# Six gathered tiles a step instead of seven in the first sweep of a graph network, and 36 counted batches in seven steps

## What is computed

```python
h = x @ L0_gnn_weight
msgs = norm[:, None] * h[src]                  # norm = deg_inv_sqrt[src] * deg_inv_sqrt[dst]
x = _layernorm(x + segment_sum(msgs, dst) + bias)

w_ij = mlp(edge_attr_64, rad_...) + mlp(edge_attr_32, sph_...)
q, k, v = (x @ wq)[dst], (x @ wk)[src], (x @ wv)[src]
alpha = (q * w_ij * k).sum(head) / sqrt(16) * edge_weight
x = _layernorm(x + segment_sum(alpha * v, dst) / 16)
```

## Time and profile before

| | |
|---|---|
| time, median of 3 runs | 1648.03 us (1643.97 to 1650.68) |
| profiled execution, its time | 1645.99 us |
| its span, first to last instruction | 1643.9 us |
| granted TensorE clock, mean | 0.986 |
| busy: PE, PEld | 1533.4 us (93%), 1418.8 us (86%) |
| busy: DVE, ACT, POOL | 1440.4 us (88%), 952.6 us (58%), 1195.5 us (73%) |

### The profile page before, as it was taken

One profiled execution on the slowest core, in us unless ns is written; L12 is line 12 of the kernel. 1 busy time (PEld: TensorE's weight loads), 2 busy tenths in 40 slices (PEclk: granted clock), 3 DMA queues, 4 the chain that ended last, 5 costly groups with the idle time before them and its releaser, 6 DMA issues.

```text
span 1643.9 us, 42998 instructions
## 1 busy us (share of the span) xinstructions
PE 1533.4 (93%) x12636; PEld 1418.8 (86%) x12636; DVE 1440.4 (88%) x4930; ACT 952.6 (58%) x1406; POOL 1195.5 (73%) x1202
## 2 busy tenths in 40 slices
PE   3499999999999869999999999999999999999996
PEld 3378988889898758999999999999999999998995
DVE  8999879798887548999999999999998999998998
ACT  3345657556565655655666666556666556655654
POOL 5777777777777357777777777777777777777772
PEclk9999999999999979999999999999999999999998
DMA  4134334343433366667667666666666666677764
GB/s 126 44 102 117 104 111 123 104 117 105 116 105 104 104 199 185 186 191 190 185 186 188 190 184 187 184 185 191 186 188 184 186 184 188 185 182 188 190 192 122
DMA packets 170086, 258.34 MB, mean 157 GB/s; under 512 B 70300, under 2 KB 84477, under 8 KB 169740
## 3 DMA queue, kind: packets, MB, share of 16 engines
q0 software_dynamic: 50240, 129.44, 29.0%
q1 hardware_dynamic: 116364, 124.61, 26.8%
q10 hardware_dynamic: 3264, 1.64, 0.3%
HBM read 232.76 MB, written 22.79 MB: 155 GB/s over the span
## 4 chain that ended last, share of the span: by engine, by line
PE 55%; DVE 18%; POOL 10%; issue 9%; DMA 3%; DVEq 2%; ACT 2%; SPq 0%; POOLq 0%; ACTq 0%
PE bank L1110 26%; PE bank L1118 11%; PE bank L1092 7%; POOL arena L811 5%; POOL arena L799 5%; DVE xsplit L1490 4%; PE bank L1149 3%; PE bank L1094 3%; DVE arena L1363 2%; DVE late L1748 2%; PE bank L1140 2%; DVE late L1738 2%; DVE red L1757 2%; DVE late L1784 2%; DVEq L1496 1%
## 5 line engine op out<-in xcount | busy, mean ns | idle before, releaser
L799 POOL DMA_INDIRECT arena<-kv_d,idx x808 | 783.4, 970 | 277.8 <-issue 273.5
L1110 PEld LDWEIGHTS bank<-w,hid 128*128 128x128 f32 x6464 | 782.8, 193 | 28.6 <-issue 3.2
L1110 PE MATMUL bank<-w,hid 128*128 128x128 f32 x6464 | 792.4, 276 | 1.0 <-ACT bank L899 1.0
L915 ACT ACTIVATE hid<-bank,b 128x512 f32<-128x512 f32 x808 | 500.2, 683 | 235.5 <-PE bank L1094 226.9
L811 POOL DMA_INDIRECT arena<-xs_d,idx x358 | 351.6, 982 | 114.5 <-issue 109.6
L1092 PE MATMUL bank<-xsplit,w_hi 128*128 128x512 f32 x808 | 344.6, 437 | 22.9 <-DVE xsplit L1490 21.0
L1490 DVE TENSOR_TENSOR xsplit<-xraw,xsplit 64x128 fp32r<-64x128 f32 x1616 | 347.1, 281 | 9.2 <-ACT xsplit L907 3.0
L1118 PE MATMUL bank<-onehot,late 128*128 128x126 f32 x1616 | 215.3, 281 | 15.2 <-DVE late L1784 14.2
L907 ACT ACTIVATE xsplit<-xraw 64x1024 fp32r<-64x1024 f32 x202 | 210.8, 1044 | 20.1 <-DMA xraw<-in_sph_t 18.8
L1118 PEld LDWEIGHTS bank<-onehot,late 128*128 128x128 f32 x1616 | 192.1, 192 | 23.9 <-DVE late L1784 22.7
L899 ACT ACTIVATE bank<-b_full 128x512 f32<-128x512 f32 x199 | 119.3, 599 | 158.4 <-DVE late L1784 156.8
(11 more groups left out here) (163 smaller groups left out, 1366.5 us busy)
## 6 DMA issues: line engine op xcount, KB each, us to landing
xraw<-in_rad_t SPq DMA_DIRECT2D x207, 128.0 KB
xraw<-in_sph_t SPq DMA_DIRECT2D x414, 64.0 KB
late<-relrow_d SPq DMA_DIRECT2D x103, 256.0 KB
w_sb<-w_d SPq DMA_DIRECT2D x52, 256.0 KB
w_d<-w_sb SPq DMA_DIRECT2D x51, 256.0 KB
arena<-kv_d,idx POOLq DMA_INDIRECT x808
arena<-xs_d,idx POOLq DMA_INDIRECT x358
qwin<-q_d SPq DMA_DIRECT2D x101, 31.5 KB
```

What stands on the lines that cost most here:

```text
L799: pool.indirect_dma_start(gath[:, k, t * width:(t + 1) * width], None, table, bass.IndirectOffsetOnAxis(ap=idx[:, pair.slot(4), j * TILES ...
L915: act.activation(hid[:, s.slot(2), c, :], hid_ps[s.sub(4, c, 4 * s.total).slot(len(hid_ps))][:, :], ACT.Silu, bias=b0[:, c:c + 1]).then_in ...
L1110: mm = pe.matmul(w_ps[:, t * D:(t + 1) * D], hid[:, b, c, t * P:(t + 1) * P], w1[:, c, :], start=False, stop=(c == 3), skip_group_check=True)
```

## The change

Every step gathers six tiles and the last one four: 304 gathered tiles. The other 504 are counted, in 252 batches: exactly seven tables of 36. Seven steps make one turn, with five batches in each and six in the seventh; products stand in steps 7, 14, ... 49, all of three full spans. Steps 49 and 50 count nothing, and the end of step 50 has no product. The arithmetic on rows that the second sweep needs (`rows_of_sweep2`, five instructions) moves ahead of the last window. In the first sweep the low halves are made in four pieces of 256 columns. The table of offsets (`coff`) shares its place with the hidden activations. The clears of the last table are spread over the last two steps.

```diff
-CLOSE = 8
-GATHERED = 7
+CLOSE = 7
+GATHERED = 6
+SHORT = 2
...
-    COLS1 = UNITS * GATHERED + 1
+    COLS1 = UNITS * GATHERED - SHORT
...
-        coff = sb("coff", [P, DENSE])
...
+        coff, _ = part(digits, 4 * GE, DENSE)
...
         def tiles1(s):
-            return GATHERED + (1 if s.is_last() else 0)
+            return GATHERED - (SHORT if s.is_last() else 0)
...
         def batches(s):
-            if s.is_last():
+            if s.is_last(2):
                 return []
-            return [Step(9 * (s.c // 2) + 4 * (s.c % 2) + j, 9 * s.unroll // 2, s.i, s.p, COUNTED)
-                    for j in range(4 + s.c % 2)]
+            turn, at = divmod(s.c, CLOSE)
+            return [Step(SPANS * SPAN_BATCHES * turn + 5 * at + j, p=s.p, total=COUNTED)
+                    for j in range(6 if at == CLOSE - 1 else 5)]
...
         def product(s):
-            if s.is_last():
-                return Step(PRODUCTS - 1, p=s.p, total=PRODUCTS)
             if s.c and s.c % CLOSE == 0:
-                return Step(s.c // CLOSE - 1, s.unroll // CLOSE, s.i, s.p, PRODUCTS)
+                return Step(s.c // CLOSE - 1, p=s.p, total=PRODUCTS)
             return None
...
# ScalarE, clear_counts
-                    for j in range(OPEN if k and k.is_last() else SPANS if k else 0):
-                        if min(c + j, max(c, UNITS - 2)) != s.c:
+                    for j in range(SPANS if k else 0):
+                        if (c + (0, 0, 1)[j] if k.is_last() else c + j) != s.c:
                             continue
...
# TensorE, sum1 and sweep1
-                for j in range(2):
+                for j in range(2 if tiles1(s) > TILES else 1):
                     pe.wait_ge(s_gath1[2 * s.slot(RING1) + j], gathered1(s, j))
...
                 if s.is_last():
-                    layer2(s, mlp1, w1_ps[0], range(2))
+                    layer2(s, mlp1, w1_ps[0])
                     sum1(s)
-                    layer2(s, mlp1, w1_ps[0], range(2, 4))
-                    pe.wait_ge(s_acc1, s.tick + 1)
-                    pe.wait_ge(s_zero, s.p * CLEARS + CLEARS - OPEN)
-                    sum_spans((s.p + 1) * COUNTED, s.p)
                     return
                 layer1(s + 1, mlp1)
-                count_batch(own[0])
+                for batch in own[0:1]:
+                    count_batch(batch)
                 if product(s):
                     pe.wait_ge(s_acc1, s.tick)
-                    sum_spans(own[0].tick, s.p)
-                count_batch(own[1])
+                    sum_spans(s.p * COUNTED + (product(s).c + 1) * SPANS * SPAN_BATCHES, s.p)
+                for batch in own[1:2]:
+                    count_batch(batch)
...
# VectorE, split_lo
                 for m in range(2):
-                    for t in range(TILES):
-                        own = slice(t * P, (t + 1) * P)
+                    width = GE // 2 if mlp is mlp1 else P
+                    for t in range(GE // width):
+                        own = slice(t * width, (t + 1) * width)
                         last = dve.tensor_tensor(xsplit[RAD:P, b, m, own], xraw[:, k, m, own],
                                                  xsplit[0:RAD, b, m, own].bitcast(F32), ALU.subtract)
...
# VectorE, sweep1
                 if s.is_last():
                     bases = load(base1_i, s.n, 1, NP - 1)
-                    span_bases = load(span_i, (product(s) * SPANS).n, SPANS, NP - 1)
+                    rows_of_sweep2(s.p)
                     dve.wait_ge(s_acc1, s.tick)
                     add_window(bases[0], WIN, sum1_ps, s_sum1, s.tick + 1, s_acc1, s.tick)
-                    rows_of_sweep2(s.p)
-                    dve.wait_ge(s_acc1, s.tick + 1)
-                    add_spans(product(s), span_bases)
                     return
...
                     if own:
                         more_hots(own[0])
-                        if not s.is_last(2):
-                            split_lo(s + 2, mlp1)
-                        dve.wait_ge(s_sum1, s.tick)
-                        one_hot(s + 1, GATHERED, tiles1(s + 1)).then_inc(s_hot1, 1)
+                        split_lo(s + 2, mlp1)
+                    dve.wait_ge(s_sum1, s.tick)
+                    one_hot(s + 1, GATHERED, tiles1(s + 1)).then_inc(s_hot1, 1)
                     dve.wait_ge(s_acc1, s.tick)
                     add_spans(product(s), span_bases)
```

More of the change, by code:

```diff
@@ L455, in tiles1 @@
         def tiles1(s):
-            return GATHERED + (1 if s.is_last() else 0)
+            return GATHERED - (SHORT if s.is_last() else 0)
         def gathered1(s, j):
-            return (s.turn(RING1) + 1) * 16 * (TILES - j) + (16 if j and s.is_last() else 0)
+            return (s.turn(RING1) + 1) * 16 * (TILES - 2 * j) - (16 * SHORT if j and s.is_last() else 0)
         def batches(s):
-            if s.is_last():
+            if s.is_last(2):
                 return []
-            return [Step(9 * (s.c // 2) + 4 * (s.c % 2) + j, 9 * s.unroll // 2, s.i, s.p, COUNTED)
-                    for j in range(4 + s.c % 2)]
+            turn, at = divmod(s.c, CLOSE)
+            return [Step(SPANS * SPAN_BATCHES * turn + 5 * at + j, p=s.p, total=COUNTED)
+                    for j in range(6 if at == CLOSE - 1 else 5)]
         def span_of(b):
@@ L748, in _ @@
                                     mid_row.unsqueeze(2).to_broadcast([P, PAIRS, 2 * TILES]), ALU.subtract))
-            most = UNITS * GATHERED
+            most = (UNITS - 1) * GATHERED
             step(pool.tensor_tensor(far1[:, 0:most].rearrange("p (g t) -> p g t", t=GATHERED),
                                     dst_f[:, 0:most].rearrange("p (g t) -> p g t", t=GATHERED),
-                                    mid_row1.unsqueeze(2).to_broadcast([P, UNITS, GATHERED]), ALU.subtract))
-            v = step(pool.tensor_tensor(far1[:, most:COLS1], dst_f[:, most:COLS1], mid_row1[:, UNITS - 1:UNITS],
-                                        ALU.subtract))
+                                    mid_row1[:, 0:UNITS - 1].unsqueeze(2).to_broadcast([P, UNITS - 1, GATHERED]), ALU.subtract))
+            v = step(pool.tensor_tensor(far1[:, most:COLS1], dst_f[:, most:COLS1],
+                                        mid_row1[:, UNITS - 1:UNITS].to_broadcast([P, COLS1 - most]), ALU.subtract))
             assert v == SET.rel, v
@@ L765, in spans @@
                 return t[:, 0:rest].rearrange("p (k t) -> p k t", t=LEN)
[L767 to L770, removed]
+            v = step(pool.tensor_tensor(spans(coff), spans(tile_f), spans(tile_f)[:, :, 0:1].to_broadcast([P, whole, LEN]),
+                                        ALU.subtract))
             step_wait(v)
@@ L773, in _ @@
             assert v == SET.coff, v
-            step(pool.tensor_copy(span_f[0:1, 0:whole], spans(tile_f)[0:1, :, 0]))
-            v = step(pool.tensor_copy(span_f[0:1, whole:PRODUCTS * SPANS],
-                                      tile_f[0:1, rest:rest + 1].to_broadcast([1, PRODUCTS * SPANS - whole])))
+            v = step(pool.tensor_copy(span_f[0:1, 0:whole], spans(tile_f)[0:1, :, 0]))
             assert v == SET.spans, v
@@ L832, in _ @@
                 pool.wait_ge(s_acc1, p * UNITS + UNITS)
-                start_over(s_gath1, [16 * (TILES - j) * len(range(b, UNITS, RING1)) + (16 if j and b == (UNITS - 1) % RING1 else 0)
+                start_over(s_gath1, [16 * (TILES - 2 * j) * len(range(b, UNITS, RING1)) - (16 * SHORT if j and b == (UNITS - 1) % RING1 else 0)
                                      for b in range(RING1) for j in range(2)], s_again[0])
@@ L1918 @@
     near = 7
-    coff = 10
-    spans = 12
-    w0 = 15
+    coff = 9
+    spans = 10
+    w0 = 13
 class CAST:
```

11 lines of the change are left out of this document (6 added, 5 removed).

## The result

| | before | after |
|---|---|---|
| median | 1647.33 us of 20 runs (1643.30 to 1650.68) | 1649.47 us of 20 runs (1646.77 to 1651.22) |
| span of the profiled execution, clock | 1643.9 us, 0.986 | 1644.7 us, 0.988 |

The ratio is 1.0015, with a 95% interval of 1.0009 to 1.0021: 2.5 us slower, 1.5 to 3.5, and within the 0.5% that stood for no change. The forecast was 1652.

A forecast was written before the change was run, and what follows sets the result against it. TensorE and GpSimd were taken to set the first sweep's turn, VectorE some 3 us behind. The profiled 1645.99 plus 2.8 (later restart) and 2.5 (SP's queue) gave 1651.3, stated as 1652 us; range 1639 to 1665.

The forecast's parts named there:

- What bounds the turn: First sweep after the change: VectorE sets the turn at 64.3 us, above TensorE's 62.2 and GpSimd's 54.2.
- the window: VectorE, last count added ahead of a product to first after it: 11.20 us, taken as unchanged.
- 36 x 0.26: TensorE's turn: 36 counting batches at 0.26 us each, 9.4 us of its 62.2.
- the rival in which the two engines keep holding each other through two banks: First sweep, VectorE and TensorE counts: VectorE keeps its waits, turn 67.1, kernel 1668 us; chance 0.20.
- TensorE sets the turn: Rival, first sweep: VectorE 2.1 us a turn cheaper, turn 62.2, kernel 1641 or 1639 us; chance 0.15.
- Halves: First sweep, VectorE: low halves in four pieces take 1.40 us instead of 1.74, 0.34 saved a step.
- The rival of whole lengths: First sweep, VectorE: each piece pays its whole length, 0.59 less a step, kernel 1642 us; chance 0.05.
- First and seventh turn: First sweep: first turn's last count at 153.3; seventh turn 2.6 us shorter, last count at 536.5.
- The end of the sweep: From last product, ending at 545.0, to VectorE's restart at 559.5: restart 2.8 us later than before.
- VectorE waits for the last clear: End of first sweep: ScalarE's third clear lasts until 14.2 us after the last product; VectorE restarts at 14.5.
- SP's queue: Passage to second sweep: SP's first loads 7.2 us behind VectorE, costing 2.5 us, between 0 and 7.2.
- Sum: Whole kernel: profiled 1645.99 plus 2.8 for the restart and 2.5 for SP, 1651.3; forecast 1652 us.

The follow-up runs named there:

- e7: Changed kernel with the six-batch step's one-hots moved into the product's window and the first sweep's low halves in one piece: ratio 0.9993, turn 63.44 us.
- e9: Changed kernel with one-hots moved into the product's window, low halves in one piece, and TensorE's batch 3 between two quarters of layer 2: ratio 0.9989.
- e5: Changed kernel without SP's first loads for a further pass of the first sweep and the waits for them: ratio 1.0020 (1.0010 to 1.0030).

## Why the forecast came out

*What bounds the turn: right, with a rival's mechanism in it.* VectorE sets it, at 63.88 against 64.3 forecast; GpSimd dropped out, the waits for tiles went, and the window kept its 11.2. But TensorE's own turn, put at 62.2, is 63.4 even where VectorE is ahead of it (e7). The term that was mis-sized is "36 x 0.26": the batches cost 10.4 there and 10.8 in the changed kernel, not 9.4. That is the rival in which the two engines keep holding each other through two banks; I looked for it as waits of VectorE, and it came as waits of TensorE, covered because VectorE was as slow. It is why three ways of taking work from VectorE (one piece, moved one-hots, both) gave 0.2, 0.2 and 0.4 us a turn instead of 1.2 and more, and why the rival *TensorE sets the turn* at 62.2 could not come about: not even e9 gets there.

*Halves.* Four pieces take 334.27 - 332.81 = 1.46 to the next instruction, against 1.74 for eight: 0.28 a step saved where I put 0.34; undoing it cost 0.25. The rival of whole lengths falls. The rule of the Trainium skill, VectorE: DVE Perf Modes, section The TRN2 errata - SBUF-src ops pay a fixed extra latency per instruction, made 0.63 of it: this case's rows contradict that for pieces in a row (0.28), while the length of a single 64x256 piece, 414 ns in the groups by line, agrees within 3% with an estimated (256 + 151) / 0.96 = 424 by that page's formula.

*First and seventh turn.* The first turn's last count fell at 153.76 (153.3). The seventh saved about 1.1, not 2.6: its last count at 536.03 is 51.56 behind its first at 484.47, where the others took 52.4 to 53.1. VectorE waited 0.89 and 1.13 for TensorE's counts there, so TensorE did set the end of that step, as forecast (timeline of VectorE after); but its last three batches took 535.49 - 534.11 = 1.38 even so, which my 0.26 each had left out.

```profile
532.63 0.47 DVE L1525 TENSOR_TENSOR count<-count,bank 128x300 f32 x1 [0.89 <-PE bank L1137]
534.67 0.47 DVE L1525 TENSOR_TENSOR count<-count,bank 128x300 f32 x1 [1.13 <-PE bank L1137]
...
536.03 0.47 DVE L1525 TENSOR_TENSOR count<-count,bank 128x300 f32 x1 [0.21 <-DVE count L1525]
```

That the last count came within 0.5 of the forecast 536.5 is in part luck: six turns were 2.5 shorter together, the first ended 0.5 later, and the seventh saved 1.5 less.

*The end of the sweep.* The product ended at 544.83 (545.0) and VectorE restarted at 559.11 (559.5), 2.4 later than before where I had put 2.8. The step "VectorE waits for the last clear" held up to there, with a wait of 2.74, but it was not the last to hold VectorE: the row that it then wanted came only at 559.57, through GpSimd's start-over and the first projection, which I had called early enough. By these rows the two ways end within half a microsecond of each other, so shortening one alone would have given back at most that; no run tried it.

*SP's queue.* The step that was mis-sized most. SP came with its first loads at 564.92 (566.5), 5.8 behind the restart where I had put 7.2, and the kv stores went out at 576.33 (575.8), yet the 2.5 us that I charged did not come: the passage took as long as before, 601.94 - 559.57 = 42.4 against 599.19 - 556.80 = 42.4. The lag shows in the first gather at most, and taking SP's loads out changed nothing in time: 2.5 us less would have made a ratio of 1.0000, below the interval of e5.

*Sum.* 2.8 and 2.5 were forecast, 2.5 (1.5 to 3.5) came. SP's 2.5 are excluded by e5; that the rest is the restart's delay follows by subtraction alone, since no run moved the restart by itself. What I did not see at all is how a delay at the start of the second sweep reaches the end: through whichever comes later, the steps or the gathers that need 20.3 us for a step of 20.0. It is shown that late gathers cost time by themselves, and late steps too, and that the steps' delay is covered when the gathers are late. That SP's queue (indices, then features behind them) is what passes it on to ScalarE is read from the waits and was not tried by itself. Nor did the runs settle all of the batches' extra 1.0 to 1.5 us a turn: about half is named as a wait for an addition, spreading three batches took 0.24 off the mean turn, and where the rest lies stays open.

## What to carry to other kernels

When an engine drops out as the bound, the time to look at is that of the next two together: here two engines that hand buffers to each other through a ring of two were slow together, and the sum of TensorE's own pieces, 62.2, came out below what any run reached (63.2). Work moved into another engine's wait gained little here (0.2 us a turn), since the buffers came back no sooner. And a shift of some microseconds between two phases is priced by the stream that comes last in the second phase, here the gathers or the steps, and not by the restart of the first engine alone.

## What the runs showed of the hardware

- One counting batch alone takes TensorE 0.26 us at the median, and two side by side 0.41 at the least and 0.53 at the median; a third in a row, which needs the first one's bank, makes it 1.38 to 1.57 in the changed kernel. The way there and back through an addition of 0.47 thus adds 0.60 or more to 3 x 0.26.
- Additions of 128x300 that wait for each other through a semaphore follow at 0.68 us, 0.21 of it standing; with one-hots between them this wait does not show.
- GpSimd's gathers of the second sweep take 0.946 us each at the median and about 1.27 from one to the next, and in the changed kernel the view names nothing but GpSimd's own issue ahead of 792 of 808: from the first to the last they took 1023 to 1030 us in every kernel, whatever the steps did.
